# Six buffers for the residual rows, and their load moved to an earlier place in SyncE's queue

## What is computed

```
x = x + tanh(g_xattn) * xattn(layernorm(x), ctx, ctx, W, b, mask)
x = x + tanh(g_ffn) * ffn(layernorm(x))

xattn: 16 heads of 16; scores = q k^T / 4, causal and padded keys at -inf, softmax, times v, then @ W.T + b
ffn:   shared = swiglu(x @ w_in.T) @ w_out.T
       routed = sum over the two chosen of 8 experts: (swiglu(x @ w1.T) * weight) @ w2[e].T
```

## Time and profile before

| | |
|---|---|
| median of three runs | 1267.52 us (1267.03 to 1269.57) |
| the profiled execution, its own time | 1266.31 us |
| its span, first to last instruction | 1264.6 us |
| TensorE's mean granted clock | 0.934 of full speed |
| busy: PE / DVE / POOL / ACT | 86% / 68% / 41% / 37% of the span |

### The profile page before, as it was taken

One profiled execution on the slowest core, in us unless ns is written; L12 is line 12 of the kernel. 1 busy time (PEld: TensorE's weight loads), 2 busy tenths in 40 slices (PEclk: granted clock), 3 DMA queues, 4 the chain that ended last, 5 costly groups with the idle time before them and its releaser, 6 DMA issues.

```text
span 1264.6 us, 21889 instructions
## 1 busy us (share of the span) xinstructions
PE 1091.2 (86%) x7027; PEld 906.5 (72%) x7027; DVE 858.1 (68%) x1865; ACT 464.5 (37%) x722; POOL 512.7 (41%) x614
## 2 busy tenths in 40 slices
PE   2669878877878889778879887999999899999997
PEld 1557766766767667667658666788888788888886
DVE  7668576757666666677577575754754478777776
ACT  2556434544444445345444444222322111111110
POOL 3333245335434533634534424320000256666664
PEclk7889888989989889889889898999999999999999
DMA  5895534545455446445444441046766355455552
GB/s 116 177 181 109 132 73 105 124 88 116 104 97 133 95 94 130 101 87 123 87 116 110 76 126 35 35 158 220 258 209 201 114 166 160 148 162 156 159 156 82
DMA packets 117339, 161.81 MB, mean 128 GB/s; under 512 B 32170, under 2 KB 82156, under 8 KB 117230
## 3 DMA queue, kind: packets, MB, share of 16 engines
q1 hardware_dynamic: 105454, 122.39, 40.4%
q0 software_dynamic: 11776, 38.03, 9.9%
HBM read 76.39 MB, written 52.12 MB: 102 GB/s over the span
## 4 chain that ended last, share of the span: by engine, by line
PE 46%; issue 25%; DVE 15%; POOL 9%; ACT 2%; SPq 2%; DMA 2%; POOLq 0%; DVEq 0%; ACTq 0%
PE ps L764 14%; PE ps L811 11%; PE ps L709 6%; PE ps L813 6%; POOL x L1477 3%; PE ps L796 3%; DVE st L989 2%; PE ps L631 2%; DVE mneg L1225 2%; POOL tab_dram L1501 2%; POOL gl L1415 2%; DVE x L1254 1%; DVE regr L997 1%; DVE regr L1233 1%; PE ps L640 1%
## 5 line engine op out<-in xcount | busy, mean ns | idle before, releaser
L811 PE MATMUL ps<-regr,gh 128*128 x600 | 222.6, 410 | 0.1
L889 ACT ACTIVATE Pt<-ps,pbias 77x1024 f32<-77x1024 f32 x128 | 141.2, 1103 | 85.0 <-PE ps L619 75.7
L813 PE MATMUL ps<-regr,gl 128*128 x600 | 169.3, 282 | 0.0
L1477 POOL TENSOR_TENSOR x<-x,regf 128x512 f32<-128x512 f32 x32 | 40.7, 1273 | 258.7 <-DMA x<-in_x 258.6
L631 PE MATMUL ps<-Pt,regf 77*32 77x256 f32 x1024 | 80.3, 441 | 72.0 <-DVE regr L997 44.8
L811 PEld LDWEIGHTS ps<-regr,gh 128*128 128x128 f32 x600 | 113.8, 190 | 25.2 <-issue 0.5
L981 ACT ACTIVATE gh<-ps 128x512 fp32r<-128x512 f32 x75 | 44.6, 598 | 205.9 <-PE ps L796 112.5
L1225 DVE TENSOR_REDUCE mneg<-ps 128x8 f32<-128x616 f32 x128 | 100.2, 792 | 23.6 <-PE ps L588 14.0
L709 PE MATMUL ps<-x2h,winh 128*128 128x512 f32 x256 | 114.9, 449 | 0.5 <-DVE OHR L1096 0.5
L813 PEld LDWEIGHTS ps<-regr,gl 128*128 128x128 f32 x600 | 114.5, 191 | 0.0
L631 PEld LDWEIGHTS ps<-Pt,regf 77*32 77x32 f32 x1024 | 31.2, 119 | 109.2 <-DVE regr L997 62.1
(11 more groups left out here) (207 smaller groups left out, 2722.1 us busy)
## 6 DMA issues: line engine op xcount, KB each, us to landing
regr<-regr SPq DMA_DIRECT2D x192, 128.0 KB, 4.8
y_dram<-Pt SPq DMA_DIRECT2D x64, 256.0 KB, 2.2
regf<-in_x SPq DMA_DIRECT2D x32, 256.0 KB, 4.8
x<-in_x SPq DMA_DIRECT2D x32, 256.0 KB, 6.0
y_dram<-res SPq DMA_DIRECT2D x32, 256.0 KB
regr<-regr SPq DMA_DIRECT2D x192, 38.5 KB, 2.1
x_dram<-x2h SPq DMA_DIRECT2D x14, 512.0 KB, 3.0
x_dram<-x2l SPq DMA_DIRECT2D x14, 512.0 KB, 3.8
```

Source lines behind the costliest of these rows:

```text
L811: e.matmul(o, gh2[:, k % 3, fc, :], w2v[:, bass.ds(val, 1), fc, :, :].rearrange("p o h d -> p (o h) d"), start=fc == 0, stop=False, skip_g ...
L813: m = e.matmul(o[:, 0, :], gl2[:, k % 3, fc, :], w2v[:, bass.ds(val, 1), fc, 0, :].rearrange("p o d -> p (o d)"), start=False, stop=fc == ...
L889: e.activation(Pt[0:K, 4 * k:4 * k + 4, :].rearrange("k (n j) t -> k n (j t)", n=2), bank_of["sc", b, k][0:K, :, :], ACT.Exp, bias=pbias[: ...
L1477: e.tensor_tensor(x1[:, b % 5, :, :], x1[:, b % 5, :, :], brow[:, :].unsqueeze(1).broadcast_to([P, 2, D]), ALU.add).then_inc(s["xb"], 1)
```

## The change

The residual rows get six buffers in place of five. Their load stands in slot 5 of its step in all steps, which is ahead of the transfers of the maxima (494) and of the queries (491) of the same step. It then waits for the ffn's result of batch b-6. The marks get one buffer in place of two, so that their load waits for the pick of the pair just before, and an integer tile of the second phase (`nti`) is laid over `lgT`.

```diff
+NX = 6
@@ phase_one
         put(i - 2, (..., (8, "values", 0), (8, "values", 1),
-                    (5 if i < 6 else 11, "load_x1", 0), (11, "att", 0)))
+                    (5, "load_x1", 0), (11, "att", 0)))
@@ build
-        pk = sb("pk", [P, 2, G, 2, K])
+        pk = sb("pk", [P, G, 2, K])
-        x1 = sb("x1", [P, 5, 2, D])
+        x1 = sb("x1", [P, NX, 2, D])
-        nti = sb("nti", [NC, 2, P], I32)
+        nti = lgT[0:NC, 0:2 * P].bitcast(I32).rearrange("c (n p) -> c n p", n=2)
@@ sync, load_kv(b)
                     e.wait_ge(s["tabw"], 32)
-                    if b >= 2:
-                        e.wait_ge(s["pick"], 3 * (b - 1))
+                    e.wait_ge(s["pick"], 3 * b)
@@ sync, load_x1
-                    if b >= 5:
-                        e.wait_ge(s["res"], b - 4)
-                    e.dma_start(x1[:, b % 5, :, :], ...).then_inc(s[f"xr{b % 5}"], 16)
+                    if b >= NX:
+                        e.wait_ge(s["res"], b - NX + 1)
+                    e.dma_start(x1[:, b % NX, :, :], ...).then_inc(s[f"xr{b % NX}"], 16)
```

More of the change, by code:

```diff
@@ L425, in load_kv @@
                     e.wait_ge(s["tabw"], 32)
-                    if b >= 2:
-                        e.wait_ge(s["pick"], 3 * (b - 1))
-                    e.dma_start(pk[:, h, :, :, :].rearrange("p g n k -> p (g n k)"),
+                    e.wait_ge(s["pick"], 3 * b)
+                    e.dma_start(pk[:, :, :, :].rearrange("p g n k -> p (g n k)"),
                                 mdr[b * G:b * G + G].rearrange("g n k -> (g n k)").partition_broadcast(P)).then_inc(s[f"kf{h}"], 16)
@@ L499, in sync @@
                         e.wait_ge(s["mt1"], 16)
-                    if b >= 5:
-                        e.wait_ge(s["res"], b - 4)
-                    e.dma_start(x1[:, b % 5, :, :], A["x"][b].rearrange("(t p) d -> p t d", p=P)).then_inc(s[f"xr{b % 5}"], 16)
+                    if b >= NX:
+                        e.wait_ge(s["res"], b - NX + 1)
+                    e.dma_start(x1[:, b % NX, :, :], A["x"][b].rearrange("(t p) d -> p t d", p=P)).then_inc(s[f"xr{b % NX}"], 16)
                 elif stage_ == "store_x2":
@@ L1179, in vector @@
                     e.wait_ge(s["mk"], 16)
-                    e.tensor_scalar(pk[:, 0, :, 0, :], mk0, 1.0, None, ALU.is_equal).then_inc(s["mark"], 1)
+                    e.tensor_scalar(pk[:, :, 0, :], mk0, 1.0, None, ALU.is_equal).then_inc(s["mark"], 1)
                     e.wait_ge(s["mark"], 1)
                     e.wait_ge(s["gcon"], GCON["ramp"])
-                    e.scalar_tensor_tensor(kone[:, :, 0, :], pk[:, 0, :, 0, :], -1000.0, ramp.unsqueeze(1).broadcast_to([P, G, K]),
+                    e.scalar_tensor_tensor(kone[:, :, 0, :], pk[:, :, 0, :], -1000.0, ramp.unsqueeze(1).broadcast_to([P, G, K]),
                                            ALU.mult, ALU.add).then_inc(s["mark"], 1)
@@ L1187, in vector @@
                     e.wait_ge(s["mark"], 3)
-                    e.tensor_tensor(pk[:, 0, :, 1, :], kone[:, :, 0, :], best[:, :].unsqueeze(2).broadcast_to([P, G, K]),
+                    e.tensor_tensor(pk[:, :, 1, :], kone[:, :, 0, :], best[:, :].unsqueeze(2).broadcast_to([P, G, K]),
                                     ALU.is_equal).then_inc(s["mark"], 1)
@@ L1204, in vector @@
                     v = kf[:, :, :].rearrange("p (g c) k -> p g c k", g=G)
-                    e.tensor_tensor(kone[:, :, :, :], v, pk[:, h, :, 1, :].unsqueeze(2).broadcast_to([P, G, 2, K]),
+                    e.tensor_tensor(kone[:, :, :, :], v, pk[:, :, 1, :].unsqueeze(2).broadcast_to([P, G, 2, K]),
                                     ALU.mult).then_inc(s["pick"], 1)
@@ L1209, in vector @@
                     e.wait_ge(s["pick"], 3 * b + 2)
-                    e.copy_predicated(v, pk[:, h, :, 0, :].bitcast(I32).unsqueeze(2).broadcast_to([P, G, 2, K]),
+                    e.copy_predicated(v, pk[:, :, 0, :].bitcast(I32).unsqueeze(2).broadcast_to([P, G, 2, K]),
                                       kfirst[:, :, :].unsqueeze(3).broadcast_to([P, G, 2, K])).then_inc(s["pick"], 1)
@@ L1253, in vector @@
                     e.wait_ge(s["xb"], b + 1)
-                    e.scalar_tensor_tensor(x1[:, b % 5, :, :], bank_of["pj", b, 0][:, :].rearrange("p (t n) -> p t n", t=2),
-                                           tg[:, 0:1], x1[:, b % 5, :, :], ALU.mult, ALU.add).then_inc(s["x1"], 1)
+                    e.scalar_tensor_tensor(x1[:, b % NX, :, :], bank_of["pj", b, 0][:, :].rearrange("p (t n) -> p t n", t=2),
+                                           tg[:, 0:1], x1[:, b % NX, :, :], ALU.mult, ALU.add).then_inc(s["x1"], 1)
                     e.wait_ge(s["x1"], b + 1)
-                    moments(x1[:, b % 5, :, :], 1, b)
+                    moments(x1[:, b % NX, :, :], 1, b)
                 elif stage_ == "norm2":
@@ L1262, in vector @@
                     for t in range(2):
-                        i = e.tensor_scalar(xn2[:, t, :], x1[:, b % 5, t, :], mv[:, 1, t, 0:1], rs[:, 1, t:t + 1],
+                        i = e.tensor_scalar(xn2[:, t, :], x1[:, b % NX, t, :], mv[:, 1, t, 0:1], rs[:, 1, t:t + 1],
                                             ALU.subtract, ALU.mult)
@@ L1306, in vector @@
                     e.scalar_tensor_tensor(res[:, hb, :, :], bank_of["so", b, hb][:, :].rearrange("p (t n) -> p t n", t=2),
-                                           tg[:, 2:3], x1[:, n % 5, :, :], ALU.mult, ALU.add).then_inc(s["res"], 1)
+                                           tg[:, 2:3], x1[:, n % NX, :, :], ALU.mult, ALU.add).then_inc(s["res"], 1)
                 elif stage_ == "route":
@@ L1475, in gpsimd @@
                         e.wait_ge(s["dcon"], DCON["brow"])
-                    e.wait_ge(s[f"xr{b % 5}"], 16 * (b // 5 + 1))
-                    e.tensor_tensor(x1[:, b % 5, :, :], x1[:, b % 5, :, :], brow[:, :].unsqueeze(1).broadcast_to([P, 2, D]),
+                    e.wait_ge(s[f"xr{b % NX}"], 16 * (b // NX + 1))
+                    e.tensor_tensor(x1[:, b % NX, :, :], x1[:, b % NX, :, :], brow[:, :].unsqueeze(1).broadcast_to([P, 2, D]),
                                     ALU.add).then_inc(s["xb"], 1)
```

## The result

The changed kernel takes 1143.57 us in the median of four runs (1142.27 to 1146.82). The kernel before takes 1267.28 us in the median of its four. The ratio is 0.903, with a 95% interval of 0.9001 to 0.906, a gain of 124 us. The profiled execution took 1144.04 us with a span of 1142.3 us.

A forecast was written before the change was run, and what follows sets the result against it. The prediction took the first phase as bound by a loop of late residual load, bias and maxima. Its 8.1 us ceiling a pair, cut to 5.7, gave 74 us over 13 pairs: 1193 us, range 1163 to 1235.

The forecast's parts named there:

- The place, the wait and who waits behind it: First phase: load issued 21 us sooner, POOL's bias wait gone in 26 steps, so DVE's line 1254 starts sooner.
- the signs named: Profile if right: no bias wait for the load, pair 41 to 44 us, clock above 0.95, TensorE about 90% busy.
- The sum: First phase: 8.1 us ceiling a pair cut to 5.7 at 90% TensorE busy; 74 us over 13 pairs.
- The ceiling: First phase: 5.8 + 2.3 = 8.1 us a pair, 105 us over 13 pairs, if nothing else is late next.
- The step that I gave 2.3 us: Step where line 1254 waits 2.66 us: TensorE's gaps of 1.63 and 0.67 us go, 2.3 us gained.
- The step that I gave 5.8: Step with DVE's 3.82 us wait: values' matmuls 3.6 us sooner plus 2.2 us from full clock.
- The clock: TensorE behind the two gaps: full clock expected instead of half rate, 2.2 us of the 5.8 by rows alone.
- the marks, the alias and the end: Marks' load, `nti` laid over `lgT`, and loads of batches 30 and 31: no effect on time expected.
- A: Scores' new wait for the maxima's transfer, 1.5 us a step, takes back 39 us: 1232 us; 19 in 100.
- C: Moved load delays the maxima's transfer by 5.2 us a step: 61 us slower, 1328 us; 3 in 100.
- D: DVE's wait passes whole to another input or the next instruction: no gain, 1267 us; 3 in 100.
- B: POOL's bias holds a DVE instruction 1.29 us in each of 26 steps, 34 us back: 1227 us; 6 in 100.

The follow-up runs named there:

- slot 10: Kernel before, residual load moved from slot 11 to slot 10 from step 6 on, ahead of its step's queries but behind the maxima's transfer: 1143.41 us, ratio 0.903.
- doubled: First sixteen matmuls of the values issued twice from batch 4 on: 1271.44 us in the kernel before, 1140.58 us in the changed one.
- fivefold matmuls: Kernel before with the first sixteen matmuls of the values issued five times from batch 4 on: 1343.44 us, ratio 1.0596.

## Why the prediction was wrong

**The place, the wait and who waits behind it: right.** The bias's wait of 258.6 us fell to 8.8, DVE's of 109.1 to none. The load in slot 11 again brings both back. Of the signs named, a pair of 41 to 44 us came for the longer kind only.

**The sum: the step that failed.** The step is the share of TensorE that I put in. I took a ceiling of 8.1 us for a pair and cut it to 5.7, since I did "not believe 95%" of TensorE busy in this phase and took "the point between, 90%". Measured is 9.0 us for a pair (112.6 us in 12.5 pairs), and 94% busy. The pair that I had worked out at 48.1 us takes 38.3, 9.8 less. TensorE's work was about right: 38.2 us estimated, 37.5 and 38.5 busy in the two kinds of pairs. The 90% had no row behind it: I argued from five engines handing work around, and measured is 98% in the shorter kind of pair and 92% in the longer. With the ceiling in place of the cut the forecast would have been 1162 us, still 18 us off.

**The ceiling was none.** It was made from the gaps of TensorE behind the wait, one step at a time. The runs show a loop: each microsecond of lateness beyond 0.9 costs a microsecond in each step. By that the sum is short: issue 3.8 plus landing 1.8, less 0.9, is 4.7 us a step, 122 us in 26 steps. That is no forecast, since the slack is fitted to the times. The issue was in the trace of before; the 4.2 us of landing in slot 10 and the slack were not. The step that I gave 2.3 us, the one with the smaller wait, gained 4.5 (23.1 to 18.6), perhaps since the maxima of the step before were earlier too; no run separates this. The step that I gave 5.8 gained 5.2.

**The base: too small.** I multiplied a pair of the shorter kind, the shortest of all, 48.1 us. The mean of the 25 steps is 49.8 a pair (622.0 us in 12.5 pairs), so up to 1.7 us a pair, 21 us in all, were missing from what there was to gain.

**The clock: about right.** I had 13 x 2.2 = 29 us. The matmuls' busy time fell by 35.1 us. Whether this is time gained or only goes with it stays open: the doubled and the fivefold matmuls did not raise the clock. Where it fell, the prediction said loosely ("behind the gaps of 1.11 and 2.48 us"). The windows of the kernel before between the rows that it read are:

```profile
409.00:411.00 2.00, 1.07 (x16) 0.50 (x16) 1.93 (x7) 0.05 (x1) 1.99 (x2) 1.00 0.06 9
411.00:413.00 2.00, 0.00 (x0) 0.00 (x0) 1.93 (x5) 1.11 (x2) 1.68 (x4) 0.62 0.02 1
```

After the gap of 1.11 us the clock was still 1.00; it fell within the gap of 2.48 us.

**Nothing for the marks, the alias and the end: right** within 3 us by the medians (5 at the end of the interval), and 3.9 us behind batch 29.

**The rivals.** A (a wait for the maxima's transfer) did not come: line 619 waited for it 2.3 us, once. Its margin was larger than I gave: the landing counts from the start of the issue, so the transfer was there at 392.16 + 2.1 = 394.3, and 2.2 us were free, not 1.5. C (landings of the maxima's transfer delayed): the profile has no landings of line 494; the nearest, line 482's, have a median of 2.1 us as before, longest 6.0. D did not come. B came in its mechanism: line 1148, beside the bias from 349.57 to 350.88, took 1.55 us, and its longest is 1859 ns where before none of the sixteen was over 481. Line 1044, six of whose nine run beside the bias, has a median of 1484 ns, where before it had 236:

```profile
L1148 DVE TENSOR_TENSOR regr<-regf,regr x16: 461/478/1859, 8.2 to 592.1; 128x308 fp32r<-128x308 f32 x16
L1044 DVE TENSOR_TENSOR e<-LGe,mx x9: 191/1484/1492, 137.5 to 693.4; 128x64 f32<-128x64 f32 x7, 128x32 f32<-128x32 f32 x2
```

The prediction said that DVE had mostly reads of PSUM to do there and passed over line 1148, which reads SBUF twice; six of the sixteen are long. Over the whole run VectorE's busy time rose from 858.1 to 882.3 us with the same 1865 instructions, 24 us, against the 34 of rival B. In slot 10 it is 870.5 us, 12 less, and the kernel takes the same time (1143.41 us). The bias is later there too, so what B costs in time stays open.

## What to carry to other kernels

Where a late transfer waits behind others whose issue itself depends on the work that the transfer delays, it is a loop: count the links of it, issue time and landing of everything ahead, times the number of rounds, and not only the idle gaps that the trace shows at one place. The slack has to be taken off, and only runs with the transfer at several places show it. What bounds the kernel next is not read from the busy shares: TensorE was busy more than VectorE, and it was the work added to VectorE that cost time. One run with a few added instructions on each engine shows it, and it is to be read for each kind of step by itself. The smallest edit that takes the transfer out from behind the others (one slot's place, no new buffer) brought everything here.

## What the runs showed of the hardware

Matmuls were added to a TensorE that was busy 94% of a stretch, up to 98%, without any cost in time over the whole kernel. A residual load of 256 KB landed in 4.2 us in the median ahead of the queries' copies (slot 10), in 5.3 behind three of these copies of 128 KB, and in about 6 behind five or six; in the changed kernel, right behind the 256 KB of line 443, its median is 5.8:

```profile
DMA to landing us min/median/max: 2.7/5.8/8.8
```

TensorE's granted clock was 1.00 after an idle gap of 1.11 us and 0.62 and then 0.50 over and behind one of 2.48 us. A DVE instruction of 0.47 us with two operands in SBUF took 1.55 us where a GpSimd instruction of 1.31 us had started 0.1 us before it. The Trainium skill, page "SBUF — State Buffer", section "SBUF: two separate sides", says that such a pair shares one port and that the one that starts second waits for the whole of the first; the rows of this pair agree, 1.2 us of waiting (349.68 to 350.88) and some 0.35 of work.
